# Causal masking of eleven of sixteen attention heads moved from TensorE to GpSimd

## The reference

```python
scores = jnp.einsum('bkgqd,bkpd->bkgqp', qg, k) * scale     # 16 heads, 4 key/value heads, D = 64
causal = jnp.tril(jnp.ones((s, s), dtype=bool))
scores = jnp.where(causal, scores, jnp.float32(-1e+30))
probs = jax.nn.softmax(scores, axis=-1)
out = jnp.einsum('bkgqp,bkpd->bkgqd', probs, v)
```

## Time and profile before

| | |
|---|---|
| median of three runs | 1931.47 us |
| profiled execution | 1928.46 us |
| its span | 1926.5 us |
| TensorE matmul busy | 1761.5 us, 91% |
| VectorE busy | 1439.4 us, 75% |
| ScalarE busy | 999.4 us, 52% |
| GpSimd busy | 693.0 us, 36% |
| mean granted TensorE clock | 0.964 of full |

### The profile page before, as it was taken

The page is one execution under the profiler, slowest core; times in us unless marked ns, Lnnn a source line. Parts: engine busy times, 40 slices in busy tenths (PEclk is TensorE's granted clock), DMA queues, the critical chain, the costliest instruction groups (busy, mean ns, idle before and its releaser), DMA issues.

```text
span 1926.5 us, 27319 instructions
## 1 busy us (share of the span) xinstructions
PE 1761.5 (91%) x9228; PEld 1426.0 (74%) x9228; DVE 1439.4 (75%) x2652; ACT 999.4 (52%) x2158; POOL 693.0 (36%) x717
## 2 busy tenths in 40 slices
PE   6678879999999969999999969999999996999998
PEld 3567767777877857777787767777787785777777
DVE  4468878887478777887568887888746888788754
ACT  1132456777441436767633426677734144777752
POOL 0023244544224144553324134444323314455422
PEclk9889989999999989999999988999999998999999
DMA  6320054343160053443161024435225005354311
GB/s 248 137 109 1 19 152 116 100 127 78 41 257 1 1 132 105 127 105 89 45 230 55 1 69 123 106 100 138 57 87 209 1 1 132 104 136 119 88 29 50
DMA packets 90127, 184.14 MB, mean 96 GB/s; under 512 B 28991, under 2 KB 43135, under 8 KB 86790
## 3 DMA queue, kind: packets, MB, share of 16 engines
q1 hardware_dynamic: 82694, 168.77, 29.9%
q10 hardware_dynamic: 7296, 13.63, 2.5%
HBM read 125.46 MB, written 46.94 MB: 89 GB/s over the span
## 4 chain that ended last, share of the span: by engine, by line
PE 70%; DVE 11%; ACT 5%; issue 4%; DMA 3%; POOL 2%; DVEq 2%; ACTq 1%; SPq 1%; POOLq 0%; another core or an unknown queue 0%
PE ps L436 10%; PE ps L559 8%; PE ps L579 7%; PE ps L581 6%; PE ps L602 6%; PE ps L600 6%; PE ps L599 6%; PE ps L442 5%; PE ps L772 4%; PE ps L693 3%; PE ps L648 3%; DVE oT L1199 2%; PE ps L585 2%; PE ps L514 1%; DMA mix<-inverse_scratch 1%
## 5 line engine op out<-in xcount | busy, mean ns | idle before, releaser
L1178 DVE CUSTOM_DVE_ANT_0 ps<-ps,mrow 128x128 f32<-128x128 f32 (+7 forms) x512 | 384.9, 765 | 115.2 <-PE ps L559 113.5
L1450 POOL TENSOR_TENSOR psplit<-pT,psplit 128x384 fp32r<-128x384 f32 (+3 forms) x320 | 301.9, 957 | 424.1 <-ACT psplit L893 419.0
L893 ACT ACTIVATE psplit<-ps 128x512 fp32r<-128x512 f32 (+3 forms) x768 | 373.1, 486 | 0.0
L892 ACT ACTIVATE pT<-ps 128x512 f32<-128x512 f32 (+3 forms) x512 | 256.3, 501 | 167.3 <-PE ps L585 88.0
L559 PE MATMUL ps<-khl,qhh 128*128 128x512 f32 (+3 forms) x768 | 252.3, 393 | 60.2 <-DMA qhh<-psplit 34.1
L579 PE MATMUL ps<-qhh,khl 128*128 128x512 f32 (+3 forms) x768 | 271.1, 353 | 7.8 <-ACT psplit L893 7.5
L581 PE MATMUL ps<-q,k 65*128 65x512 f32 (+3 forms) x768 | 267.9, 349 | 0.0
L599 PE MATMUL ps<-psplit,vhi 128*65 128x512 f32 (+3 forms) x768 | 264.0, 344 | 0.0
L602 PE MATMUL ps<-psplit,vhi 128*65 128x512 f32 (+3 forms) x768 | 259.5, 338 | 0.0
L600 PE MATMUL ps<-psplit,vlo 128*65 128x512 f32 (+3 forms) x768 | 259.0, 337 | 0.0
L559 PEld LDWEIGHTS ps<-khl,qhh 128*128 128x128 f32 x768 | 131.6, 201 | 79.3 <-issue 59.6
(11 more groups left out here) (200 smaller groups left out, 3305.1 us busy)
## 6 DMA issues: line engine op xcount, KB each, us to landing
qhh<-q_scratch SPq DMA_DIRECT2D x112, 256.0 KB, 4.9
q_scratch<-hrow SPq DMA_DIRECT2D x24, 1024.0 KB, 6.9
mix<-inverse_scratch SPq DMA_DIRECT2D x64, 256.0 KB, 3.5
q<-q_scratch SPq DMA_DIRECT2D x56, 256.0 KB, 4.3
Kf<-kf_scratch SPq DMA_DIRECT2D x3, 3072.0 KB, 17.3
khl<-k_scratch SPq DMA_DIRECT2D x24, 256.0 KB, 7.5
sgn<-sgn_scratch SPq DMA_DIRECT2D x6, 1024.0 KB, 10.0
x<-in_x SPq DMA_DIRECT2D x5, 1024.0 KB, 5.4
```

The costliest lines, as they stand in the source:

```text
L892: A(full(n)[:, 0:hi - lo], ps[:, b, 0:hi - lo], ACT.Exp, scale=SCALE)
L893: A(psplit[:, n % PRING, 0, 0:hi - lo], ps[:, b, 0:hi - lo], ACT.Exp, scale=SCALE)\
L1178: V.tensor_tensor_reduce(out=v, in0=v, in1=mrow[:, L - n:L], scale=1.0, scalar=-3e38, op0=ALU.add, op1=ALU.max, accum_out=mx[:, u % 2, i:i ...
L1450: G.tensor_tensor(psplit[:, n % PRING, 1, 0:m], full(n)[:, 0:m], psplit[:, n % PRING, 0, 0:m].bitcast(F32), ALU.subtract)\
```

## The change

A constant `QUIET` names heads 1, 2, 5, 6 and 9 to 15, the eleven without projections. In these, `score_cols` leaves the mask matmul L585 out, so the exponentials are taken of unmasked scores. After the low part of a diagonal block has been made, GpSimd sets the forbidden part of the first 128 columns to zero in both parts at once, with one `affine_select` over 128 partitions by 2 x 128 elements of `psplit`. It waits for the low part's semaphore, its own (`low_pool`) in seven of the eight diagonal blocks and VectorE's (`low_dve`) in (1,4). `values` then waits for this selection before its first matmul, where before it waited for the exponential, and for the low part only ahead of the third. A semaphore `masked_done` is added. Heads 0, 3, 4, 7 and 8 stay as they were.

```diff
+QUIET = (1, 2, 5, 6) + tuple(range(9, HEADS))
...
+        def masked(u, c, j):
+            return u in QUIET and j >= 4 * c
+
+        def mask_made(u, j):
+            return at("masked_done", NT * QUIET.index(u) + j + 1)
...
-                diagonal = j * P >= c * HALF
+                diagonal = j * P >= c * HALF and not masked(u, c, j)
...
-                pe.wait_ge(*at("exp_done", n + 1))
+                if masked(u, c, j):
+                    pe.wait_ge(*mask_made(u, j))
+                else:
+                    pe.wait_ge(*at("exp_done", n + 1))
...
-                pe.wait_ge(*low_made(n))
+                if not masked(u, c, j):
+                    pe.wait_ge(*low_made(n))
...
+            def mask(u, c, j):
+                n = NBLK * u + 4 * c + j
+                pool.wait_ge(*low_made(n))
+                v = psplit[:, n % PRING, :, 0:P]
+                G.affine_select(out=v, in_=v.bitcast(F32), compare_op=ALU.is_ge, fill=0.0, base=0,
+                                pattern=[[0, 2], [1, P]], channel_multiplier=-1).then_inc(s["masked_done"], 1)
...
                         if (c, j) in POOL_LOW:
                             score_low(u, c, j)
+                        if masked(u, c, j):
+                            mask(u, c, j)
```

More of the change, by code:

```diff
@@ L87 @@
         "w1_split": 2, "x_done": 1, "tap_made": 1, "edge_done": 6, "gates_mixed": 1, "bias_added": 6, "y_pool": 3,
-        "causal_made": 1, "rope_done": 8, "v_done": 4, "low_pool": 112, "x_loaded": 16,
+        "causal_made": 1, "masked_done": NT * len(QUIET), "rope_done": 8, "v_done": 4, "low_pool": 112, "x_loaded": 16,
         "gates_loaded": 16, "first_rows0": 64, "first_cols": 64, "first_rows1": 64, "m_loaded0": 128,
@@ L304, in adaln_hyena_binffn_gqa_moe @@
                  "m_loaded1", "v_copied",
-                 "exp_done", "causal_made", "low_pool", "low_dve", "pv_done", "o_done", "sum_loaded", "inverse_done",
+                 "exp_done", "causal_made", "masked_done", "low_pool", "low_dve", "pv_done", "o_done", "sum_loaded", "inverse_done",
                  "inverse_stored", "inverse_loaded", "oT_done", "top_done", "w1_loaded0", "w1_loaded1",
```

## The result

The kernel after takes 1941.18 us (1936.62 to 1951.52, 14 runs), the kernel before beside it 1931.56 us (1927.72 to 1938.51). The ratio is 1.0047, with a 95% interval of 1.0033 to 1.0061: some 9 us slower. The forecast of 1932 was no change. The time lies inside the range, but the case that came true was slower by over 0.3%.

What follows compares the result with a forecast made beforehand. Heads without projections were taken as bound by TensorE, 14.06 us each. Each sequence gains 3.6, loses 0.55, gains 0.55 and loses 3.7: 0.1 us lost, 0.4 in four sequences, giving 1932 us on the median, range 1914 to 1950.

Steps and rivals of the forecast that it cites:

- the case that came true: Whole kernel slower by over 0.3% (5.8 us), given a chance of 0.32.
- likeliest case: Whole kernel near 1932 us, within 0.3% (5.8 us), that is no change; chance 0.37.
- The price of the selection: GpSimd: 0.40 us each, starting 0.16 behind its low part, lengthening the cluster by 0.56, ends 0.40 and 0.95.
- The loop: Heads 10 to 14: chain through GpSimd's low parts and masks, ScalarE and VectorE sets a period of 13.95 us, 13.5 to 14.3.
- the collision: VectorE's low part of (1,0) stalls GpSimd's low part of (0,2) by up to 0.69 us, some 0.5 beyond slack.
- wrong in kind: Stated signs of failure: TensorE waits for the selection early in a head, or its waits lower its clock.
- The rival that TensorE stays the bound: Collisions fall into slack, heads 10 to 14 gain 0.72 us each, 13 us in all, 1918 us; chance 0.31.
- The exclusion: Rival: GpSimd stands still whenever VectorE reads two SBUF operands; heads 14.5 us, 11 us lost, 1943 us; chance 0.22.
- The relief: TensorE: each removed mask saves 0.11 us, lower bound 0.06; 0.72 us a head after a wait for VectorE's maximum.
- The gain of heads 1, 2, 5, 6 and 9: Beside projections: 0.72 us each, 3.6 a sequence; lateness from heads 2 and 6's one full cluster dies in the projection behind.
- The wait in head 2: TensorE's wait ahead of L559, read as a DMA for the next group's queries and keys, eats 0.55 us a sequence.
- The last head: Head 15: masks delay the exponential of (1,0) by 1.9 us and the end by 1.8, losing 3.7 a sequence.

Runs made afterwards that it cites:

- The relief alone: Kernel after with the selection on GpSimd and the wait for it left out, so eleven heads aren't masked at all: 1919.85 us, 0.9913 of the kernel before.
- twice the price: Kernel after with a second selection of the same size, over a dead tile, ahead of each: 2025.72 us, 1.0460 of the kernel before.
- the two orders of six: Kernel after, selecting only in heads 5, 6, 9 to 13, blocks (1,4) to (1,7) plus (0,2), (0,3): 1920.60 us; or plus (0,0), (0,1): 1919.24 us.
- the first kernel with six blocks: Kernel after, selecting only in heads 5, 6, 9 to 13, blocks (0,2), (0,3) and (1,4) to (1,7): 1920.60 us, 0.9943 of the kernel before.

## Why the prediction was right in its range and wrong in its likeliest case

**The price of the selection** held. 0.41 us for 0.40, starting 0.08 behind the low part for 0.16, so 0.49 us for 0.56, well inside the ends 0.40 and 0.95.

**The loop** came out in size: heads 9 to 14 at 13.84 us for 13.95, between 13.5 and 14.3, with ScalarE's (1,0) waiting for L1461 as named. The relief alone gives 13.43 and twice the price 16.1, so GpSimd sets it. That the collision does part of it is likely: the period falls to 13.56 when the selections take 0.407 instead of 0.484 on average, but the number of selections changes with it, so the two aren't told apart. Where the loop closes I had wrong, as the two orders of six show. TensorE waits for the selection of (0,3), 0.40 us at 892.02: I had named such a wait early in a head as a sign of being wrong in kind. Whether the loop closes through it isn't shown. (The low part of (0,1), given as 893.80, is 893.84 by its own terms; that moves nothing.) The rival that TensorE stays the bound gave 13.34 and fell here. The exclusion (14.5) fell as well: VectorE's operations strike 56 of the 352 selections, one or two of the eight in heads 9 to 14, not the whole cluster. The Trainium skill (GPSIMD Engine Reference, Key points) has GpSimd contend with VectorE's instructions of two SBUF inputs. The trace agrees as far as it says there is contention, 0.94 for 0.41 us; the period doesn't bear out a full sum of both engines.

**The relief** was mis-sized: 0.61 us a head for 0.72, or 0.076 for each mask, between my 0.11 and my bound of 0.06. The Trainium skill (TensorE: Matmul & The Clock Gate, LDWEIGHTS) would give 0.107 for a load of 128 columns. That is more than leaves the path here.

**The gain of heads 1, 2, 5, 6 and 9**, "5 x 0.72 = 3.6", is the step that failed by most. The six stretches 0 to 1, 1 to 2, 4 to 5, 5 to 6, 6 to 7 and 8 to 9 hold 32 of these heads' 40 masks. With my prices of 0.11 for a mask, less 0.16 in each first half, they had to gain 2.7 us. They gained 0.9. (The other eight lie in 2 to 3 and in 9 to 10.) Two things were wrong besides the price of a mask. First, GpSimd takes back what TensorE gains around head 6: 5 to 6 takes 13.75 us for 13.40 with the relief alone, and 6 to 7 takes 16.64 for 16.12, 0.9 us together. I had written that the lateness of one full cluster "dies in the projection behind". It doesn't. With only the second half selected it is nearly all back, 13.58 and 16.13. Second, the relief isn't there at all in 4 to 5 and in 8 to 9, where I had 0.28 us each. I had read TensorE as the bound from one stretch in heads 10 and 11 and carried it behind the projections, although 4 to 5 with its 15.04 us against 14.05 was in the trace of before. What holds that stretch stays open. In 1 to 2 the full relief came (13.46, with and without selections); why there and not in 5 to 6 stays open too.

**The wait in head 2** was priced as a transfer that eats 0.55 us. The stretch with it cost 1.37 in place of gaining: the wait itself got longer (1.73 to 2.34 us for 1.26 to 1.90, 2.10 for 1.48 on average, so by 0.6 as priced), and in all four sequences TensorE fell to half its clock behind it, which I hadn't priced. The earlier trace rows showed the longest of the four, 1.90, and it was the one with the lower clock behind it. I had not looked at the granted clock of the next microseconds, only written that I would be wrong in kind if waits lowered it. The kernel with heads 1 and 2 alone shows the step by itself, and the count over all kernels (16 of 16 for 12 of 32) bears it out.

**The last head** was right as a mechanism and a little large. In the kernel after, the end of the second sequence reads as follows. (The rows ahead of the prediction, from about 712 to 966 us, are of the second sequence too and not of the third: the records show four attentions, which start near 257, 708, 1162 and 1616 us in the kernel before.)

```profile
967.48 0.41 POOL L1468 TENSOR_SCALAR_AFFINE_SELECT psplit<-psplit 128x256 fp32r<-128x256 f32 x1
```

```profile
957.34 0.60 ACT L903 ACTIVATE pT<-ps 128x512 f32<-128x512 f32 x1 [1.01 <-PE ps L613]
...
968.38 0.59 ACT L911 ACTIVATE work<-ps 65x512 f32<-65x512 f32 x1 [3.22 <-PE ps L613]
```

Head 14's records are at 947.46 and, before, 939.86. The exponential of (1,0) lies 9.88 behind it for 8.32, +1.56 for the 1.9 forecast, and the last copy of the sum 20.92 for 17.56, +3.36 for 3.7. Of this 0.7 hides (+2.63 at the last scaling), where up to 0.9 was allowed. Head 14's selections make 1.05 of the 3.36, as the kernels with and without them show, and those of head 15's second half 1.70.

**The sum.** Forecast for each sequence: -3.6, +0.55, -0.55, +3.7. Measured: -0.9 (the six stretches above), +1.37 (2 to 3), -1.05, +2.63, with -0.3 elsewhere, 1.7 lost. Two errors pull the loop and the end in my favour by 1.6 us, and the two failed steps cost 3.5. That makes 1.7 for 0.1, and with four sequences 6.9 for 0.4 us. That the time came so near is in part luck: the first two errors make up for nearly half of the other two. The range was wide enough, the likeliest case wasn't the right one.

## What to carry to other kernels

An engine is the bound only in the heads in which it was shown to be: measure the period of every head by a record that it has once, before multiplying one head's saving by their number. Count, too, which of the removed operations lie between two such records: here a stretch holds halves of two heads. Work taken from a busy engine and added to an idle one is paid at each place where nothing runs behind it, here the end of each sequence, and where the relieved engine then waits for a load. Move it only in the heads and blocks that have slack: seven heads and six blocks gave 1920.6 us where eleven and eight gave 1941.2.

## What the runs showed of the hardware

GpSimd's selection has a single input in SBUF and still takes 0.94 instead of 0.41 us when it starts 0.02 us behind VectorE's low part of two operands, which keeps its 0.69 (889.56 in the kernel after). So not only GpSimd's two-input operations are held. The reverse occurs as well: a selection that starts 0.10 us ahead of VectorE's low part keeps its 0.41, and VectorE's takes 0.84 for 0.69 (909.88 in the first kernel with six blocks), and L1210 behind a selection took 1.42 for 1.22. But the one that starts first isn't always spared: the low part on GpSimd at 797.19 started 0.35 us ahead of VectorE's operation and still took 2.17 us for 0.735.

Over all kernels but the one with twice the price, TensorE's waits in head 2 of up to 1.43 us were followed by a stretch at the full clock (2 to 3 in 18.1 to 18.3 us), all of 2.10 and more by a slowed one (19.9 or more). From 1.47 to 2.03 us both occur: 1.73 in the kernel after was followed by the lower clock, 1.72 in the one without heads 1, 2, 14 and 15 was not. A wait of 2.34 us in place of 1.30 made the stretch 2.17 us longer (20.35 for 18.18), so about one more microsecond than the wait itself grew. A saving that lengthens such a wait can be worth less than nothing.
